# A transformer layer pair with a routed expert block: mask products over 128 rows, the gate behind tile 11, two residuals moved, less second-norm work on POOL

## The reference, cut to what matters

```
ln(x)  = (x - mean) / sqrt(var + 1e-5)                    # no gain
h      = attention(ln(x), keys, values) + ln(x)           # 16 heads of 8, relu projections
x      = x + ln(h)
z      = ln(x)                                            # input of the encoder layer
y1     = ln(z + mha(z)) * g1 + b1                         # attention over the 8 sequences, 4 heads of 32
gates  = softmax(y1 @ wg); idx = argmax(gates)            # 8 experts
keep   = a token's place in its expert's queue < 512
moe    = keep ? gate[idx] * ((y1 @ w1[idx] + b1[idx]) @ w2[idx] + b2[idx]) : 0
y2     = ln(y1 + moe) * g2 + b2
out    = x + ln(y2)
```

## Time and profile before

| | |
|---|---|
| median of 3 runs | 661.74 us |
| profiled execution, its own time | 663.98 us |
| its span, first to last instruction | 662.3 us |
| PE busy | 546.7 us (83%), 3475 matrix products |
| DVE busy | 535.4 us (81%) |
| ACT busy | 393.8 us (59%) |
| POOL busy | 219.5 us (33%) |
| mean granted PE clock | 0.906 |

### The profile page before, as it was taken

How to read it: one execution, slowest core, us unless ns; L and a number is a source line. 1 busy time by engine, 2 the same in 40 slices (tenths; PEclk the granted TensorE clock), 3 DMA queues, 4 the chain that set the end, 5 groups by cost and what they waited for, 6 DMA issues and landing times.

```text
span 662.3 us, 9804 instructions
## 1 busy us (share of the span) xinstructions
PE 546.7 (83%) x3475; PEld 195.2 (29%) x3475; DVE 535.4 (81%) x882; ACT 393.8 (59%) x773; POOL 219.5 (33%) x326
## 2 busy tenths in 40 slices
PE   2784899999999999999999987766779999898600
PEld 1560122222222222222222224645565334122100
DVE  4869799999999999999999923799775843289986
ACT  1651598998898888988889863535533001025333
POOL 7001020178034450354403660835653000014441
PEclk9996599999999999999999999979879989696555
DMA  9842010111111121211221001100000000000102
GB/s 242 256 137 112 13 40 21 41 35 52 48 60 31 34 55 46 67 27 31 59 55 53 7 10 42 38 0 2 1 1 1 0 1 0 0 0 1 32 21 75
DMA packets 31393, 28.94 MB, mean 44 GB/s; under 512 B 6240, under 2 KB 23784, under 8 KB 31344
## 3 DMA queue, kind: packets, MB, share of 16 engines
q1 hardware_dynamic: 29312, 27.33, 14.4%
q10 hardware_dynamic: 2032, 0.98, 0.6%
...
## 4 chain that ended last, share of the span: by engine, by line
PE 49%; DVE 31%; POOL 7%; ACT 6%; issue 4%; DMA 2%; ACTq 0%; SPq 0%; DVEq 0%
PE ps L1490 13%; PE ps L1485 10%; DVE row_max L1662 9%; PE ps L607 7%; PE ps L1458 5%; DVE space L948 3%; DVE space L889 2%; PE ps L605 2%; ACT attended L1610 2%; PE ps L614 2%; DVE space L275 1%; ACT space L1594 1%; PE ps L562 1%; DMA w_in<-in_L_ffn_out_proj_w 1%; DVE space L1056 1%
## 5 line engine op out<-in xcount | busy, mean ns | idle before, releaser
L1662 DVE TENSOR_REDUCE row_max<-ps 128x2 f32<-128x1024 f32 x256 | 299.5, 1219 | 16.3 <-PE ps L1458 13.5
L1594 ACT ACTIVATE space<-ps 128x512 f32<-128x512 f32 x512 | 271.7, 605 | 47.8 <-PE ps L1485 47.4
L1485 PE MATMUL ps<-space 51*128 51x512 bf16 x512 | 158.8, 387 | 6.6 <-ACT space L1594 3.3
L1490 PE MATMUL ps<-space 128*32 128x512 f32 x1024 | 138.1, 612 | 3.0 <-ACT space L1594 0.7
L1458 PE MATMUL ps<-space 48*128 48x512 bf16 x512 | 128.0, 399 | 14.2 <-DVE row_max L1662 12.5
L1485 PEld LDWEIGHTS ps<-space 51*128 51x128 bf16 x512 | 41.0, 94 | 164.6 <-ACT space L1594 144.9
L607 PE MATMUL ps<-W,space 128*128 128x512 f32 x128 | 87.3, 770 | 0.0
L1334 POOL CAST max_parts<-row_max 128x16 bf16<-128x16 f32 x32 | 6.3, 197 | 238.3 <-DVE row_max L1662 238.3
L948 DVE TENSOR_REDUCE space<-ps 128x128 f32<-128x1024 f32 x32 | 38.9, 1221 | 42.3 <-PE ps L607 42.3
L444 POOL TENSOR_TENSOR space<-PC,same_row 128x512 f32<-128x512 f32 x32 | 33.0, 1061 | 36.2 <-DVE PC L903 28.3
L454 POOL TENSOR_TENSOR space<-space,rows 128x512 f32<-128x512 f32 x24 | 30.0, 1270 | 41.1 <-DVE space L275 22.9
...
## 6 DMA issues: line engine op xcount, KB each, us to landing
...
attended_dram<-attended SPq DMA_DIRECT2D x128, 18.0 KB
...
```

The lines of the kernel that those rows point to most:

```text
L1485: pe.matmul(ps[:, col_bank(v), :], k_rows[rows_a, kappa // 4 % 2, tc * P:(tc + 1) * P], q_stack[rows_a, kappa % 4, b * S:(b + 1) * S], sta ...
L1490: mm = pe.matmul(ps[32 * m:32 * m + 32, PV, :], v_heads[:, tc, PAIR * (kappa // 4) + m % PAIR, :], probs[:, tc % 2, m, :], start=(tc == 0) ...
L1594: act.activation(probs[:, tc % 2, m, :], ps[:, col_bank(v), :], ACT.Exp, scale=1.0 / math.sqrt(DH)).then_inc(s_pr, 1)
L1662: dve.tensor_reduce(row_max[:, par].rearrange("p (a c) -> p a c", a=PAIR)[:, :, item], ring(n), AX.X, MAX).then_inc(s_free, 1)
```

## The change

Eight edits are made together:

1. `others` becomes [128, 4 groups, 4 pairs, 128], zero outside the 32 partitions of its pair, in the space of `w1T`. The mask product contracts over all 128 rows. `copy_others` is four instructions; POOL clears the tile once, in item 5 of the first attention.
2. On PE the last group's turns and route and the counts move ahead: they stand among tiles 8 to 11, and tiles 12 to 31 follow without a break. DVE's `choose(3)`, both copies and the gate move likewise.
3. On DVE, `residual(0)` moves ahead of the last group's first-attention norm, and `residual(1)` ahead of `normalise(5)`.
4. `norm_smalls` loses two instructions (the halved mean, and scale plus epsilon, which the root's scale and bias now do); `norm_invert` gains the shift, and `norm_apply` multiplies and adds.
5. POOL's `affine2` is two instructions of 1024 columns instead of four of 512, for groups 0 and 1 only; `sum_up(1)` and the residuals of groups 0 and 1 stay on POOL.
6. DVE takes `sum_up(2)`, `affine2(2)` and `last_residual(2)`.
7. The order of the tail is new on DVE, ACT and POOL.
8. SP waits for POOL's semaphore for groups 0 and 1 and for DVE's for 2 and 3.

The diff without the orders:

```diff
+others = w1T[:].rearrange("p a c d -> p (a c d)").bitcast(BF16).rearrange("p (g k t) -> p g k t", g=G, t=P)
...
-others = view(space7, 0, [G, P], BF16)
...
+eps = sb("eps", [P, 1])
...
-s_mt, s_nm = sem("masks_turned"), sem("others_ready")
+s_mt, s_nm, s_eps, s_oz = sem("masks_turned"), sem("others_ready"), sem("epsilon_set"), sem("others_cleared")
...
 def norm_smalls(dve, ch, st6, small):
- ch.done(dve.tensor_scalar(mean, mean, 0.5, None, MUL))
- ch.wait()
- ch.done(dve.tensor_tensor(var, var, small[:, 4, :], ADD))
- ch.wait()
- dve.tensor_scalar(var, var, 1.0 / D, EPS, MUL, ADD).then_inc(s_var, 1)
-def norm_invert(dve, ch, k, small):
+ ch.wait()
+ dve.tensor_tensor(var, var, small[:, 4, :], ADD).then_inc(s_var, 1)
+def norm_invert(dve, ch, k, small, ready=None):
...
 def norm_invert(dve, ch, k, small):
+ ins = dve.scalar_tensor_tensor(small[:, 4, :], small[:, 0, :], -0.5, small[:, 3, :], MUL, MUL)
+ if ready is None:
+  ch.done(ins)
+  ch.wait()
+ else:
+  ins.then_inc(ready, 1)
...
 def norm_apply(dve, src, dst, small, which=range(B)):
-  ins = dve.tensor_scalar(dst(b), src(b), small[:, 0, b:b + 1], small[:, 3, b:b + 1], SUB, MUL)
+  ins = dve.tensor_scalar(dst(b), src(b), small[:, 3, b:b + 1], small[:, 4, b:b + 1], MUL, ADD)
...
-TAIL = [(4, 0), (4, 1), (5, 0), (4, 2), (5, 1), (4, 3), (5, 2), (5, 3)]
+TAIL = [(4, 0), (4, 1), (5, 0), (5, 1), (4, 2), (5, 2), (4, 3), (5, 3)]
...
 def root(act, k, small=small):
- act.activation(small[:, 2, :], small[:, 2, :], ACT.Sqrt).then_inc(s_sd, 1)
+ act.activation(small[:, 2, :], small[:, 2, :], ACT.Sqrt, scale=1.0 / D, bias=eps[:]).then_inc(s_sd, 1)
...
 def back_end_sp(sp):
-   sp.wait_ge(s_y2, g + 1)
+   sp.wait_ge(s_y2p if g < 2 else s_y2, g + 1 if g < 2 else 1)
...
- def affine(g, gain, shift, done):
-  for row, op in ((gain, MUL), (shift, ADD)):
+ def affine1(g):
+  pool.wait_ge(s_n3, g + 1)
+  for row, op in ((0, MUL), (1, ADD)):
...
 def affine(g, gain, shift, done):
-     ins.then_inc(done, 1)
+     ins.then_inc(s_y1, 1)
...
- def affine1(g):
-  pool.wait_ge(s_n3, g + 1)
-  affine(g, 0, 1, s_y1)
- def sum_up(g):
-  pool.wait_ge(s_wa, g)
-  for lo in (0, QB):
-   half = A[:, g, lo:lo + QB]
-   ins = pool.tensor_tensor(half, half, YT[:, g, lo:lo + QB], ADD)
-   ins.then_inc(s_sum, 1)
...
 def affine2(g):
-  affine(g, 2, 3, s_aff)
- def last_residual(g):
-  pool.wait_ge(s_n5, g + 1)
-  pool.tensor_tensor(same(A[:, g]), same(A[:, g]), same(X[:, g]), ADD).then_inc(s_y2, 1)
+  ch.done(pool.tensor_tensor(A[:, g], A[:, g], bcast(rows[:, 2, :], B), MUL))
+  ch.wait()
+  pool.tensor_tensor(A[:, g], A[:, g], bcast(rows[:, 3, :], B), ADD).then_inc(s_aff, 1)
...
 def last_residual(g):
...
+ pool.wait_ge(s_wa, 1)
+ pool.tensor_tensor(same(A[:, 1]), same(A[:, 1]), same(YT[:, 1]), ADD).then_inc(s_sum, 1)
+ pool.wait_ge(s_n5, 1)
+ pool.tensor_tensor(same(A[:, 0]), same(A[:, 0]), same(X[:, 0]), ADD).then_inc(s_y2p, 1)
...
+ pool.wait_ge(s_n5, 2)
+ pool.tensor_tensor(same(A[:, 1]), same(A[:, 1]), same(X[:, 1]), ADD).then_inc(s_y2p, 1)
...
 def turned_mask(g):
- bank, lo = (5, B * E) if g < 2 else (7, 0)
+ bank, lo = (5, 5, 6, 7)[g], B * E
...
-LOGITS_BANK = [5, 5, 6, 6]
+LOGITS_BANK = [5, 5, 6, 7]
...
 def experts(k):
-  bank, rows_k, variant = expert_bank(k), slice(32 * (b // 2), 32 * (b // 2) + 32), b % 2
+  bank = expert_bank(k)
...
-   pe.matmul(ps[:, bank + half, :], others[rows_k, g, :], c_stack[rows_k, variant, cols],
+   pe.matmul(ps[:, bank + half, :], others[:, g, b // 2, :], c_stack[:, b % 2, cols],
...
 def tile(k):
-   pe.wait_ge(s_nm, k // B + 1)
+   pe.wait_ge(s_nm, QB * (k // B + 1))
...
-   pe.wait_ge(s_nm, 1)
+   pe.wait_ge(s_nm, QB)
...
+ def turn_last(half):
...
-   mm = pe.transpose(ps[:, 6 + half, b * P:(b + 1) * P], A[:, G - 1, QB * half + b, :], ident[:])
+   mm = pe.transpose(ps[:, 7 - half, b * P:(b + 1) * P], A[:, G - 1, QB * half + b, :], ident[:])
...
+ pe.wait_ge(s_lgc, 3)
...
- pe.wait_ge(s_lgc, G)
+ pe.wait_ge(s_nm, QB * 3)
...
-  act.copy(same(YT[:, G - 1, QB * half:QB * half + QB]), ps[:, 6 + half, :]).then_inc(s_y1c, 1)
+  act.copy(same(YT[:, G - 1, QB * half:QB * half + QB]), ps[:, 7 - half, :]).then_inc(s_y1c, 1)
...
 def copy_others(g):
-  dve.tensor_scalar(others[:, g, :], turned_mask(g), -1.0, 1.0, MUL, ADD).then_inc(s_nm, 1)
+  if g == 0:
+   dve.wait_ge(s_oz, 1)
+  for k in range(QB):
+   rows_k = slice(32 * k, 32 * k + 32)
+   ins = dve.tensor_scalar(others[rows_k, g, k, :], turned_mask(g)[rows_k, :], -1.0, 1.0, MUL, ADD)
+   ins.then_inc(s_nm, 1)
...
- def shift(small):
-  return dve.scalar_tensor_tensor(small[:, 4, :], small[:, 0, :], -1.0, small[:, 3, :], MUL, MUL)
...
 def scale4(g):
-  norm_invert(dve, ch, tail(4, g), small4(g))
-  shift(small4(g)).then_inc(s_i4, 1)
+  norm_invert(dve, ch, tail(4, g), small4(g), s_i4)
+ def affine2(g):
+  dve.wait_ge(s_n4, g + 1)
+  ch.done(dve.tensor_tensor(A[:, g], A[:, g], bcast(rows[:, 2, :], B), MUL))
+  ch.wait()
+  ch.done(dve.tensor_tensor(A[:, g], A[:, g], bcast(rows[:, 3, :], B), ADD))
+  ch.wait()
...
 def variance5(g):
-  dve.wait_ge(s_aff, g + 1)
...
+  if g < 2:
+   dve.wait_ge(s_aff, g + 1)
...
 def scale5(g):
-  norm_invert(dve, ch, tail(5, g), small5(g))
-  shift(small5(g)).then_inc(s_i5, 1)
...
+  norm_invert(dve, ch, tail(5, g), small5(g), s_i5)
+ def sum_up(g):
+  dve.wait_ge(s_wa, g)
+  ch.done(dve.tensor_tensor(same(A[:, g]), same(A[:, g]), same(YT[:, g]), ADD))
+  ch.wait()
+ def last_residual(g):
+  dve.wait_ge(s_n5, g + 1)
+  dve.tensor_tensor(same(A[:, g]), same(A[:, g]), same(X[:, g]), ADD).then_inc(s_y2, 1)
...
+ dve.wait_ge(s_sum, 1)
...
- dve.wait_ge(s_sum, 2)
...
- dve.wait_ge(s_sum, 4)
...
- ch.wait()
...
+ norm_invert(dve, ch, tail(4, g), small4(g), s_i4)
+ dve.wait_ge(s_i4, G)
...
- ch.wait()
- dve.wait_ge(s_n4, G)
- ch.done(dve.tensor_tensor(A[:, g], A[:, g], bcast(rows[:, 2, :], B), MUL))
- ch.wait()
- dve.tensor_tensor(A[:, g], A[:, g], bcast(rows[:, 3, :], B), ADD).then_inc(s_aff, 1)
...
+ ch.wait()
...
+ dve.wait_ge(s_i5, G)
...
 def _(pool):
+ pool.memset(eps[:], EPS).then_inc(s_eps, 1)
...
 def build(kappa):
+  if kappa == 5:
+   pool.wait_ge(s_wu, E)
+   pool.memset(others, 0.0).then_inc(s_oz, 1)
...
 def _(act):
+ act.wait_ge(s_eps, 1)
```

More of the change, by code:

```diff
@@ L743, in back_end_pe @@
             pe.matmul(ps[:, 6, T * E:2 * T * E], all_ones[:], masks, start=True, stop=True).then_inc(s_cnt, 1)
-            for k in range(20, T):
+            for k in range(12, T):
                 tile(k)
@@ L1009, in back_end_dve @@
                 select(6 if lo == 0 else 7)
-            for k in range(8, 11):
-                select(k)
+            select(8)
             choose(2)
+            select(9)
+            select(10)
+            choose(g)
+            copy_others(2)
             select(11)
-            copy_others(2)
-            for k in range(12, 20):
-                select(k)
-            choose(g)
-            select(20)
             copy_others(g)
-            select(21)
             dve.wait_ge(s_ge, 1)
```

97 lines of the change are left out of this document (48 added, 49 removed).

## The result

The changed kernel takes 625.92 us (median of 4 runs, 624.61 to 627.25); the kernel before, run beside it, 661.12 (657.94 to 662.3). The ratio is 0.9475, 95% interval 0.9434 to 0.9516.

What follows compares the result with a forecast made beforehand. It saw a PE-bound and a DVE-bound stage run in a row, separated by the gate. Span: 634.7 with the gate earlier, less 3.8 for residuals, plus 5.0 for clock, 635.9; median 635.5 us, range 628 to 648.

Steps and rivals of the forecast that it cites:

- columns streamed are unchanged: 0 to 64 x 5 ns, I take 0: Mask products on PE: 64 weight loads over 128 rows instead of 32 were taken to cost nothing.
- the clock, forecast at +5: PE from 530 to 606 us: at 1.2 GHz for one third of the time, adding 5 us.
- the clock stays high: Rival for PE's clock: no low-clock time, 630.5 us instead of 635.5; chance 0.12.
- Residuals: residual(0) and residual(1) moved earlier on DVE shorten PE's stops before projections; 3.8 us carried through.
- Norm arithmetic: Small norm instructions on DVE: two go, one comes in the plain norm; eight tail norms save 2.3 us.
- The gate earlier: Last group's gate moved among earlier tiles: ready at 552.3 us instead of 586.7.
- The ledger of DVE behind the gate: DVE from gate to its end: 63.4 us of work plus 15.3 of waits and held weighs, ending at 631.0.
- 15.3 us put back: DVE behind the gate: waits for PE tiles, POOL and ACT, and weighs caught by POOL, added to the work.
- POOL hits: Rival: POOL's affines and residuals meet DVE's small norm instructions, three more hits of 2.4 us; 642.5 us, chance 0.07.
- low half of the time: Rival: PE at low clock half the time from 530 to 606, costing 12 us instead of 5; 642.5, chance 0.10.
- residual moves hidden: Rival: moving the two residuals earlier gains nothing, +3.8 us; 639.5 us, chance 0.08.
- The slower case: Rival: PE stays at 1.2 GHz from tile 12 to the end; span 667.7, median 667 us, chance 0.05.

Runs made afterwards that it cites:

- e2: The changed kernel with mask products over 32 rows again, the operand still in its new place; 631.92 us.
- e3: The changed kernel with mask products over 64 rows instead of 128; 630.02 us.
- e10: The changed kernel with POOL's second affines of the first two groups in four instructions of 512 elements instead of two of 1024; 625.27 us.
- e4: The changed kernel with both residuals back in their old places; 628.84 us.
- e9: The changed kernel with both residuals back in their old places and the norm's old arithmetic; 631.4 us.
- e14: The changed kernel with an interleaved end, group 1's sum and POOL's remaining affines and residuals on DVE, POOL idle behind the gate; 620.31 us.

## Why the prediction was wrong

**The step that failed: "columns streamed are unchanged: 0 to 64 x 5 ns, I take 0".** The edit of the mask products was valued by how long a load and a product take, and both were about right (91 and 98 ns, 0.39 and 0.38 us). The cost was in when the load can start. The trace of the kernel before had it, in the lines shown above from 539.56 on: the loads and their products start together, and a tile takes 2.74 us, where the same products take 2.15 with equal row counts. With 32 rows the forecast's early part was right: M to G was forecast as 56.5 us (492.0 to 548.5), e2 measured 55.6, the kernel after 48.2. This term was -7.4 us instead of 0, all of it ahead of the gate, and twelve tiles at 0.59 us less are 7.1 of it. Behind the gate, where DVE sets the time, the faster tiles gave nothing (G to E 77.2 in e2, 77.3 after).

**The other step: the clock, forecast at +5.** Between 545 and 585 the kernel after was never low; windows of PE show it:

```profile
545.00:585.00 40.00, 30.84 (x82) 1.00 0.05 13
585.30:590.40 5.10, 3.75 (x7) 0.67 0.01 2
```

A third of the time at 1.2 GHz, carried over from the earlier trace rows, did not come. The rival "the clock stays high", at 630.5, had this part. The granted clock of a stretch in one execution was used as a property of the stage; the earlier trace rows showed it at either level in the same kind of work. What decides it stays open: behind the gate e2 excludes the width of the mask products, ahead of it no run does, and none tells busier PE from chance.

**The sum, by its own steps.** Span forecast 635.9, measured 625.5:

| stretch | forecast | after | difference |
|---|---|---|---|
| M (495.8 less 3.8) | 492.0 | 496.3 | +4.3 |
| M to G | 56.5 | 48.2 | -8.3 |
| G to E, without clock | 78.7 | 77.3 | -1.4 |
| clock | 5.0 | 0 | -5.0 |
| E to end | 3.7 | 3.6 | -0.1 |

The +4.3 is in part chance. The kernel after's 496.3 is a late M among the ten kernels with the residuals moved (mean 494.5), and the 495.8 from which the forecast took off 3.8 is the earliest of the six with them in place (mean 496.6). Only e2, e3 and e10, at 491.3 to 492.2, came where the forecast put M or before. A stage that scatters so can't be fixed by one trace to better than some 5 us.

**Residuals: right in mechanism, the size is not settled.** Both stops fell to 1.16 us. For the forecast 3.8 us the means of M give 2.1, and e4 gives 2.9 by medians and 0.9 by ratios. e9 and e10, run side by side, give 6.1 us for residuals and norm arithmetic together, which is what the forecast has for the two (3.8 + 2.3). **Norm arithmetic: about right**, 1.4 to 2.0 us behind the gate against 2.3. **The gate earlier: right in mechanism.** PE and DVE are both busy over 80% ahead of the gate; behind it DVE is at 85% and PE at 66%, so the mark "both over 80% from 545 to 605" was missed for PE: faster tiles made PE wait for DVE, 12.8 us behind the gate. **The ledger of DVE behind the gate: right in its sum**, 77.3 against 78.7. Its largest item, 19.0 us of small instructions and weighs held by POOL, held up in e9: 17.3 us of small ones went. The 15.3 us put back were 12.0 of waits and 3.3 of weighs held by POOL; 13.5 us of idle time came, and 3.8 of held weighs (8.7 against the 4.9 of e14). What remains as work is 60.0 us against a forecast of 63.4. Too high there was weigh(0), by 2.0 us: its eight instructions took 2.18 us, and 4.19 before. So the sum came out closer than its items. POOL's groups took 16.4 us against "some 17".

**The rivals.** "POOL hits" did not happen (small instructions 6.7 us), nor did "low half of the time"; "residual moves hidden" has the later M of the old places and e9 beside e10 against it. None of the rivals had a faster tile. The slower case needed PE at 1.2 GHz from tile 12 on; PE was at 2.4 GHz until 585.
